# One-core cross-attention and routed FFN: first product transposed, slots by a matmul per batch, units of 32 tokens on four column tiles

## What is computed

```python
x = x + _L0_xattn_ref(_layernorm(x), ctx_1024, ctx_1024, ctx_1024)
#   x1 = x @ w1.T; x2 = x @ v1.T; h = gelu_tanh(x1) * x2; return h @ w2     (w1 = v1 = w2 = ctx)
x = x + _L0_ffn_ref(_layernorm(x), router_w, w1, b1, w2, b2)
#   assign = argmax(x @ router_w); w = sigmoid(logit of assign)
#   out = (gelu(x @ w1[assign] + b1[assign]) @ w2[assign] + b2[assign]) * w
```

## Time and profile before

| | |
|---|---|
| median of 3 runs | 468.7 us (468.23 to 469.79) |
| profiled execution, its span | 468.6 us |
| TensorE busy | 315.6 us (67%) |
| VectorE, ScalarE, GpSimd busy | 93.7, 84.7, 79.0 us |
| granted TensorE clock, mean | 0.842 of 2.4 GHz |
| moved by DMA | 102.18 MB, mean 218 GB/s |

### The profile page before, as it was taken

One profiled execution on the slowest core, in us unless ns is written; L12 is line 12 of the kernel. 1 busy time (PEld: TensorE's weight loads), 2 busy tenths in 40 slices (PEclk: granted clock), 3 DMA queues, 4 the chain that ended last, 5 costly groups with the idle time before them and its releaser, 6 DMA issues.

```text
span 468.6 us, 5970 instructions
## 1 busy us (share of the span) xinstructions
PE 315.6 (67%) x1840; PEld 156.7 (33%) x1841; DVE 93.7 (20%) x289; ACT 84.7 (18%) x129; POOL 79.0 (17%) x132
## 2 busy tenths in 40 slices
PE   3797897797793359585796617628777096577871
PEld 1353453353352214331353203213334042232441
DVE  1243443443335210100111000100111011010210
ACT  2120120121020012221044002102122021040410
POOL 0000000000001310313224220320323203202241
PEclk9998988998896576987999687875989587887998
DMA  8698987988879593697718754874785555000000
GB/s 293 215 328 259 300 268 238 284 261 279 293 285 322 157 396 160 232 344 259 285 59 293 296 191 181 325 257 182 277 308 213 200 183 197 26 3 20 20 25 5
DMA packets 19762, 102.18 MB, mean 218 GB/s; under 512 B 3757, under 2 KB 4013, under 8 KB 10480
## 3 DMA queue, kind: packets, MB, share of 16 engines
q1 hardware_dynamic: 16592, 96.22, 57.9%
q0 software_dynamic: 3104, 4.94, 3.3%
HBM read 99.23 MB, written 6.04 MB: 225 GB/s over the span
## 4 chain that ended last, share of the span: by engine, by line
PE 53%; issue 22%; DMA 19%; DVE 3%; SPq 1%; POOL 0%; ACT 0%; DVEq 0%; POOLq 0%; ACTq 0%
PE bank L502 17%; DMA area<-in_ctxT_a 16%; PE bank L466 12%; PE bank L476 7%; PE bank L369 7%; PE bank L495 3%; DMA b1s<-in_b 3%; PE bank L486 2%; PE bank L397 2%; PE bank L455 2%; DMA work<-t_rows,id_tok 1%; PE bank L384 0%; PE bank L447 0%; DVE tn L602 0%; PE bank L363 0%
## 5 line engine op out<-in xcount | busy, mean ns | idle before, releaser
L466 PE MATMUL bank<-W_early,work 128*64 128x512 f32 x128 | 44.1, 852 | 40.7 <-issue 39.9
L369 PE MATMUL bank<-area,xnT 128*100 128x338 f32 (+1 forms) x128 | 54.2, 577 | 17.6 <-DMA area<-in_ctxT_a 17.0
L502 PE MATMUL bank<-W_early,work 128*64 128x256 f32 x512 | 62.1, 397 | 0.0
L809 POOL DMA_INDIRECT out<-work,at_out x21 | 21.6, 1027 | 205.5 <-DVE work L728 205.5
L476 PE MATMUL bank<-W_early,work 128*32 128x256 f32 x256 | 24.5, 495 | 45.0 <-issue 45.0
L397 PE MATMUL bank<-work,hidT 128*100 128x512 f32 (+1 forms) x96 | 47.3, 604 | 0.6 <-ACT hidT L563 0.6
L502 PEld LDWEIGHTS bank<-W_early,work 128*64 128x64 f32 x512 | 36.8, 143 | 24.9 <-issue 9.7
L737 DVE COPY work<-bank 128x256 f32<-128x256 f32 (+1 forms) x21 | 11.6, 552 | 167.5 <-PE bank L466 97.6
L369 PEld LDWEIGHTS bank<-area,xnT 128*100 128x100 f32 x128 | 25.1, 207 | 44.5 <-issue 23.0
L586 ACT ACTIVATE work<-work 128x512 f32<-128x512 f32 x21 | 13.3, 631 | 140.1 <-DVE work L741 140.1
L466 PEld LDWEIGHTS bank<-W_early,work 128*64 128x64 f32 x128 | 12.2, 195 | 67.2 <-issue 66.1
(11 more groups left out here) (95 smaller groups left out, 260.1 us busy)
## 6 DMA issues: line engine op xcount, KB each, us to landing
W_early<-in_w SPq DMA_DIRECT2D x52, 1024.0 KB, 7.0
work<-in_ctx_main SPq DMA_DIRECT2D x8, 1280.0 KB
area<-in_ctxT_a SPq DMA_DIRECT2D x8, 768.0 KB, 12.4
work<-in_w SPq DMA_DIRECT2D x6, 1024.0 KB, 9.0
area<-in_w SPq DMA_DIRECT2D x6, 1024.0 KB, 9.2
area<-in_ctxT_b SPq DMA_DIRECT2D x8, 676.0 KB, 11.5
xw_rows<-xw SPq DMA_DIRECT2D x8, 200.8 KB
area<-in_x SPq DMA_DIRECT2D x8, 200.0 KB
```

What stands on the lines that cost most here:

```text
L369: last = nc.tensor.matmul((p_xa, p_xb)[part][0:T, 0:hi - lo], xnT[:, k, :], ctxTs[part][:, k, :], start=(k == 0), stop=(k == KD - 1))
L466: last = nc.tensor.matmul(p_h[BLK * h:BLK * h + BLK, :], pairT[:, k, BLK * par:BLK * par + BLK], W1[slot][:, k, D * h:D * h + D], start=(k ...
L502: last = nc.tensor.matmul(p_y[BLK * h:BLK * h + BLK, 0:HD], hT[:, 2 * (c % 4) + c // 4, :], W2[slot][:, c, HD * h:HD * h + HD], start=Fals ...
L809: nc.gpsimd.indirect_dma_start(out_halves, bass.IndirectOffsetOnAxis(ap=at_out[par][:, :], axis=0), y_out[par], None, bounds_check=bound_x ...
```

## The change

- **First product transposed.** Context columns are stationary and the 100 tokens move (`hidden`): the product comes out as context x tokens, in the form in which `attention` needs it. The transposes of the hidden rows and their copies go.
- **Context in thirds of a ring.** `ctxT_part` and `ctx_part` have three buffers each, every one for half a batch's context. Two weight pieces stand between the loads of each batch.
- **Raw x in the rows.** Per batch one tensor `rows` takes x after attention with mean, inverse deviation and gate; each token is four pieces of 128 columns. Logits are computed from x itself with a centred router (`rc`), the gate from the logit times the inverse deviation. Units normalise after the gather.
- **Slot table by a matmul per batch.** `place_rows` writes two one-hot matrices, `slots` adds tok_hot.T x slot_hot (100 x 128 by 100 x 400) to the table in PSUM.
- **Units of 32 tokens**, each on four column tiles in both layers. A gather brings 128 pieces (32 tokens x 4), VectorE normalises them and transposes 32 x 32 blocks, also the result of the first layer (`turn`), and TensorE returns the residual by an identity. There is one form only: no branch on the size.
- **Four early units**, for experts 0 to 3, take tokens of batches 0 to 6; between them the last batch is routed. Then each expert has one unit that always runs (`must`) and further ones in a loop (`more`); all experts are unrolled.
- **Weights.** Five slots as before, in four pieces; the loads wait for release only. Biases b2 are loaded once, broadcast.

The core of the diff, in the order SyncE, TensorE, ScalarE, VectorE, GpSimd:

```diff
-EARLY = (0, 1, 1, 1, 1, 1, 2, 3)
+XS, CS = 96, 80
 SA = 3 * P
-BLK = 64
-SMALL = 32
-MAXB = E - 1 + -(-(TOK - E + 1) // BLK)
-NCOL = MAXB + 6
-NTHR = TOK // BLK
+XR = 3
+U = 32
+Q = 4
+ROW = P + 4
+EARLY = 4
 SLOTS = 5
...
+        def units_of_experts(eng, must, more):
+            begin = 0
+            for e in range(E):
+                must(e, begin)
+                end = end_of(eng, e)
+                with eng.If(end > begin):
+                    with eng.Fori(begin, end) as f:
+                        more(e, f, begin)
+                begin = end
+            return begin
...
+            early = iter([(e, piece) for e in range(SLOTS - 1) for piece in range(4)])
             for b in range(NB):
+                if 2 * b + 3 < 2 * NB:
+                    sp.wait_ge(s_xps[0], b + 1)
+                    load_ctxT(2 * b + 3)
+                load_w(*next(early))
+                if 2 * b + 4 < 2 * NB:
+                    sp.wait_ge(s_xps[1], b + 1)
+                    load_ctxT(2 * b + 4)
+                if b == 1:
+                    sp.dma_start(b1s[:, :, :], b1).then_inc(s_bias, 16)
+                    sp.wait_ge(s_b2q, 32)
+                    for j in range(Q):
+                        sp.dma_start(b2s[U * j:U * j + U], b2_q[j].unsqueeze(0).to_broadcast([U, E, P + 1])
+                                     ).then_inc(s_bias, 16)
+                if 2 * b + 3 < 2 * NB:
+                    sp.wait_ge(s_att0, b + 1)
+                    load_ctx(2 * b + 3)
+                load_w(*next(early))
+                if 2 * b + 4 < 2 * NB:
+                    sp.wait_ge(s_att, b + 1)
+                    load_ctx(2 * b + 4)
+                if b + 3 < NB:
+                    sp.wait_ge(s_x2, b + 1)
+                    load_x(b + 3)
+            sp.wait_ge(s_xps[1], NB)
+            load_w(SLOTS - 1, 0)
...
+            for e in range(SLOTS, E):
+                sp.wait_ge(s_w1_used, e - SLOTS + 1)
+                load_w(e, 0)
+                load_w(e, 1)
+                sp.wait_ge(s_w2a_used, e - SLOTS + 1)
+                load_w(e, 2)
+                sp.wait_ge(s_w2b_used, e - SLOTS + 1)
+                load_w(e, 3)
...
+            def hidden(b, c):
+                n = 2 * b + c // 3
+                if c % 3 == 0:
+                    pe.wait_ge(s_T[n % 3], t_count(n))
+                bank_c = (p_xa, p_xb)[c // 3]
+                at0 = T * (c % 3)
+                for k in range(KD):
+                    last = nc.tensor.matmul(bank_c[0:CW[c], at0:at0 + T],
+                                            ctxT_part(n)[:, k, P * (c % 3):P * (c % 3) + CW[c]], xnT[:, k, :],
                                             start=(k == 0), stop=(k == KD - 1))
+                if c % 3 == 2:
+                    last.then_inc(s_xps[c // 3], 1)
...
+            def slots(b):
+                pe.wait_ge(s_slot, b + 1)
+                nc.tensor.matmul(p_tab if b < NB - 1 else p_tab_last, tok_hot[:, :],
+                                 slot_hot[:, :, :].rearrange("p e n -> p (e n)"),
+                                 start=(b % (NB - 1) == 0), stop=(b >= NB - 2)).then_inc(s_tabps, 1)
...
+            def first_layer(v, e, first, used):
+                slot, landed = e % SLOTS, 16 * (e // SLOTS) + 16
+                pe.wait_ge(s_xT, v)
+                pe.wait_ge(s_hc, v)
                 for k in range(KD):
                     if first and k % 2 == 0:
+                        pe.wait_ge(s_w[slot][k // 2], landed)
+                    for q in range(Q):
+                        last = nc.tensor.matmul(p_h[U * q:U * q + U, 0:2 * P], xT[:, U * k:U * k + U],
+                                                W1[slot][:, k, :].rearrange("p (c q l) -> p q c l", c=KF, q=Q)[:, q],
+                                                start=(k == 0), stop=(k == KD - 1), tile_position=(0, U * q))
+                        if used and k == 0 and q == 0:
+                            last.then_inc(s_w1_used, 1)
+                last.then_inc(s_h, 1)
+                pe.wait_ge(s_rT, v)
+                pe.wait_ge(s_res, v)
+                for q in range(Q):
+                    last = nc.tensor.matmul(p_r[U * q:U * q + U, 0:P], rT[:, U * q:U * q + U], ident,
+                                            start=True, stop=True, tile_position=(0, U * q))
+                last.then_inc(s_r, 1)
...
+            def second_layer(v, e, used):
+                slot, landed = e % SLOTS, 16 * (e // SLOTS) + 16
+                pe.wait_ge(s_act, v)
+                pe.wait_ge(s_yo, v)
                 for c in range(KF):
+                    if c % 4 == 0:
+                        pe.wait_ge(s_w[slot][2 + c // 4], landed)
+                    for q in range(Q):
+                        last = nc.tensor.matmul(p_y[U * q:U * q + U, 0:P], hT[:, c, :],
+                                                W2[slot][:, c, P * q:P * q + P],
+                                                start=(c == 0), stop=(c == KF - 1), tile_position=(0, U * q))
+                        if used and c == KF // 2 and q == 0:
+                            last.then_inc(s_w2a_used, 1)
                 last.then_inc(s_y, 1)
...
+            def must(e, begin):
+                v = pe.snap(begin + (EARLY + e + 1))
+                first_layer(v, e, e >= EARLY, e > 0)
+                second_layer(v, e - 1 if e > 0 else EARLY - 1, e > 0)
+            def more(e, f, begin):
+                v = pe.snap(f + (EARLY + e + 2))
+                first_layer(v, e, False, False)
+                second_layer(v, e, False)
...
+            def gelu_unit(v, v1):
+                act.wait_ge(s_hb, v)
+                if v1 is not None:
+                    act.wait_ge(s_y, v1)
+                nc.scalar.activation(hT[:, :, :], hb[:, :].rearrange("p (c t) -> p c t", c=KF), ACT.Gelu
+                                     ).then_inc(s_act, 1)
...
+            def fetch(j, v, row, index, e):
+                nc.vector.tensor_scalar(tb[:, :], row[:, 0:P], row[:, P + 1:P + 2], row[:, P + 2:P + 3],
+                                        ALU.subtract, ALU.mult).then_inc(s_tb, 1)
+                dve.wait_ge(s_tb, v)
+                nc.vector.transpose(xT[:, :], tb[:, :]).then_inc(s_xT, 1)
+                nc.vector.transpose(rT[:, :], row[:, 0:P]).then_inc(s_rT, 1)
+                nc.vector.tensor_copy(lin[:, bass.ds(ring(j), 1)], index)
...
+            def residual(j, v, row, e):
+                dve.wait_ge(s_r, v)
+                nc.vector.scalar_tensor_tensor(out=res[:, bass.ds(ring(j) * ROW, P + 1)], in0=b2s[:, e, :],
+                                               scalar=row[:, P + 3:P + 4], in1=p_r, op0=ALU.mult, op1=ALU.add
+                                               ).then_inc(s_res, 1)
...
+            def finish(j, v):
+                dve.wait_ge(s_y, v)
+                dve.wait_ge(s_yfree, v)
+                dve.wait_ge(s_res, v)
+                at0 = ring(j) * ROW
+                to = j % 2 * P if isinstance(j, int) else dve.snap(j % 2) * P
+                nc.vector.scalar_tensor_tensor(out=y[:, bass.ds(to, P)], in0=p_y[:, 0:P],
+                                               scalar=res[:, bass.ds(at0 + P, 1)], in1=res[:, bass.ds(at0, P)],
                                                op0=ALU.mult, op1=ALU.add).then_inc(s_yo, 1)
...
+            def turn(v):
+                dve.wait_ge(s_h, v)
+                nc.vector.transpose(hb0[:, :], p_h[:, 0:KF * U]).then_inc(s_hc, 1)
+            def add_bias(v, v1, e):
+                dve.wait_ge(s_hc, v1)
+                dve.wait_ge(s_act, v)
+                nc.vector.tensor_tensor(hb[:, :].rearrange("p (h n t) -> p h n t", h=2, n=4),
+                                        hb0[:, :].rearrange("p (h n t) -> p h n t", h=2, n=4),
+                                        b1s[:, e, :].rearrange("p (n h) -> p h n", h=2).unsqueeze(3
+                                                               ).to_broadcast([P, 2, 4, U]), ALU.add).then_inc(s_hb, 1)
...
+            def must(e, begin):
+                v, j = dve.snap(begin + (EARLY + e + 1)), dve.snap(begin + (EARLY + e))
+                dve.wait_ge(s_must[e], 16)
+                at0 = NB32 * (e + 1) + (e < EARLY)
+                fetch(j, v, frow[:, e, :], tab[:, at0:at0 + 1], e)
+                finish(dve.snap(begin + (EARLY + e - 2)), v)
+                turn(v)
+                add_bias(v, dve.snap(begin + (EARLY + e + 2)), e)
+                residual(j, v, frow[:, e, :], e)
...
+            def put_out(j, v, par):
+                if isinstance(j, int):
+                    at0 = j % 4
+                else:
+                    at0 = pool.snap(j % 4)
+                pool.wait_ge(s_yo, v)
+                nc.gpsimd.tensor_copy(at[par][:, :], lin[:, bass.ds(at0, 1)]).then_inc(s_at, 1)
+                pool.wait_ge(s_at, v)
+                nc.gpsimd.indirect_dma_start(out_q, bass.IndirectOffsetOnAxis(ap=at[par][:, :], axis=0),
```

(19 more changed lines are left out.)

1170 lines of the change are left out of this document (536 added, 634 removed).

## The result

The new kernel takes **354.1 us** (median of four runs, 351.5 to 358.0) against 469.3 of the kernel before on the same chip: a ratio of **0.751, 95% interval 0.746 to 0.756**. The profiled execution has a span of 351.0 us. The forecast was 341 (312 to 382). All medians here are over all runs of a kernel, while the ratios leave out runs over 1.5% above the fastest of their kernel; by this stricter rule the medians would be 353.1 us for the new kernel, 322.3 in experiment 1, 336.7 in 3, 348.0 in 7, 321.1 in 9, and within 0.5 us of those given in the others.

A forecast was written before the change was run, and what follows sets the result against it. The prediction saw serial waits in attention and table stages, and TensorE's far branches in the units, as the bound. Attention 128, table and early units 28.5, units 154, branches 18 and tail 12 sum to 341 us, range 312 to 382.

The forecast's parts named there:

- attention stage ends: Attention stage: 41.7 MB at 340 GB/s, 123 us, plus 5 us of start, gives 128 us; bounds 116 to 155.
- to the first regular first layer: Table and early units: early gather, then VectorE's pace through four units and last routing, 28.5 us, to 156.5.
- 27 distances, undisturbed: Regular units: VectorE's chain of 5.1 us sets the period, taken as 5.5 (5.0 to 6.4); 28 units, 154 us.
- what skips add: Unit stage: eight far TensorE branches, 3.5 us less 1.3 covered by queued matmuls, 18 us; bounds 0 and 38.
- last unit and tail: End of kernel: after the last unit, second layer 1.9 plus 9.4 us, 12 with its wait.
- Forecast A: Whole kernel: the forecast sum holds, 330 to 352 us; chance 0.45.
- Rival D: Attention stage: deeper buffers don't raise the DMA rate, 276 GB/s, stage ends at 156, total 369 us; chance 0.11.
- text's signs of being wrong: First layers wait for gathers or weights, or VectorE's list after the last attention product takes over 25 us.
- C: Units: TensorE's instruction stream bounds; records at 60 ns (6.4 us a unit) and branches at 4.8, 386 us; chance 0.24.
- Weights: Weight loads: expert 5 starts at 167, eleven experts at 370 GB/s land by 292 us, hidden with some 15 us spare.
- Rival B: Units: weights bound, 307 us, beside VectorE's chain at 5.0 with branches covered, 308; interfering up to 325; chance 0.18.
- E: Units: slower than before; scatter landing of 18 us makes units over 9.7 us, total above 468.7; chance 0.02.

The follow-up runs named there:

- experiment 1: New kernel with TensorE's stream written out (known unit counts as constants, no branch, loop or count load), other engines unchanged: 325.5 us.
- experiment 3: Kernel before with only TensorE's stream written out (known blocks and sizes as constants, no branches), other engines as they were: 337.1 us, ratio 0.722.
- experiment 7: New kernel with the fifth slot's weights issued only after the gathers of the early units have landed: 351.4 us, ratio 0.746.
- experiments 9: New kernel with TensorE's stream written out, plus a spare VectorE transpose of 0.45 us behind each regular unit's first layer: 321.5 us, ratio 0.688.
- Experiment 6: New kernel with the sixteen early weight pieces moved behind the attention stage: 348.2 us, ratio 0.744.
- Experiments 2: New kernel with the streams of TensorE, VectorE, ScalarE and GpSimd all written out (known counts, no branches): 321.7 us, ratio 0.687.
- experiment 11: New kernel with TensorE's stream written out, second layers cut from 128 to 64 columns: 320.2 us, ratio 0.686.
- 12: New kernel with TensorE's stream written out, every other chunk of the second layers left out (64 fewer instructions a unit): 316.4 us, ratio 0.680.
- experiment 5: Kernel before with the block-size branch removed on all engines, every block in the 64-token form, no knowledge of the routing: 377.2 us, ratio 0.802.
- experiment 4: Kernel before with TensorE's stream written out and SyncE's four waits for landings of the previous weight halves removed: 338.2 us, ratio 0.723.

## Why the prediction was right or wrong

The sum was 128 + 28.5 + 154 + 18 + 12; taken apart at the last unit's first layer it can be laid beside the trace.

| | predicted | measured |
|---|---|---|
| attention stage ends | 128 | 130.1 |
| to the first regular first layer | 28.5 | 34.1 |
| 27 distances, undisturbed | 27 x 5.5 = 148.5 | 27 x 4.66 = 125.9 |
| what skips add | 18 | 42.0 |
| last unit and tail | 5.5 + 12 | 18.9 |

**Forecast A: 10 us short of the span, the units right by luck, with two errors that cancel.** The measured median lies 2 us above A's own range, well inside the whole one. By the distances the unit's period was sized too long by 0.84 us, and the skips at less than half: seven at 6.0 us, not eight at 2.2. -22.6 and +24.0 leave +1.4. If only what experiment 1 took away is put down to the skips, they are 27.5 (+9.5) and the rest 140.4 (-8.1): less wrong each, and cancelling as well.

**Attention stage: right in what bounds it, its end partly by luck.** 41.7 MB, full share, 359 GB/s where 340 was taken. Those 41.7 MB were moved by 119.5 us (a mean of 349 GB/s from the start), when the last part of the transposed context landed, 8.5 us before the sum's 128; then came 10.6 us of the last batch's products, which were no term of it. Experiment 6 shows the stage bound by DMA, with TensorE 11 us below (12.8 us a batch, where the sum gave 11.7). Rival D is out: the deeper buffers did raise the rate.

**Table and early units: +5.6.** The step that failed is the start: "some 3 us for the early gather". The gather reads rows from memory that the last batch has first to be written to; this write, 6.4 us behind weight pieces, was no term of the sum, and the gather took 5.65, not 3.5. From the first early unit on, 24.6 us were predicted (the terms given add up to 24.9) and 25.4 measured.

**Period: the mechanism holds for a part of the units, size off.** VectorE's list from the end of a first layer to the next tokens' transposes takes 1.8 to 2.7 us in most units and 3.5 in two, where 3.0 was summed, and the 0.4 added for control and clock wasn't needed. TensorE waits for it before 10 of the 28 first layers; others start with TensorE's own layers back to back, 3.9 us apart, or behind a stop. Experiments 2 and 9 show that it yields to others over the whole stage. Of the text's signs of being wrong, one came up once: the first layer at 210.34 waited for its gather (5.54 us, landed at 209.6), of which VectorE stood still for 1.5.

**Second layer: C's first half is out.** Its 64 records take

```profile
148.20 1.95 PE bank L398 x64
```

so four column tiles run at 30 ns a record, half of the 60 that C took, and with half the columns (experiment 11, in the timeline: start, us)

```profile
171.10 1.08 PE L409 MATMUL bank<-W_early,hT 128*32 128x64 f32 x64
```

it is the columns that set it. The Trainium skill's "TensorE: Matmul & The Clock Gate" (What happens when you issue a matmul) has about 62 ns as what the sequencer may spend on a matmul. The prediction put that figure on each of the 64 records, 4.0 us, which is out at once. That the 64 records of the whole form come to 61 ns a pair, an fp32 matmul being two, would agree; the 34 ns a pair of the half form doesn't, and decides: no such bound here.

**Skips: the term that was mis-sized, and the second half of C the nearest of the rivals.** The branch itself was foreseen, and rather lower than its 3.5 us: its 16 instances sum to 16.3 us, those of the seven skips to 14.6, 2.1 each (L239 and L226 of the earlier trace rows sum to 53 and 21). What failed is "less 1.3 that queued matmuls cover", a figure that no run shows, and the thought that the wait ends with the branch. TensorE stops again inside the next layers (2.80 us at 181.4), and the lower clock follows; since these stops go with the branches in experiment 1, the code behind the target isn't there either. The bound of 38 us for it, kept in the range, lies between the 27.5 of experiment 1 and the 42 of the distances. The rule of the Trainium skill ("Runtime: NRT & Kernel Launch", Instruction fetch mechanics) that branching breaks the sequential prefetch fits the stops at the branches and behind them. Its remark there that crossing a block is mostly hidden agrees with experiment 3, where straight code kept TensorE busy 40 of 40 us; whether the short stops of experiment 1, in straight code too, are such crossings no run here shows.

**Weights: hidden, as said, and later.** They land at 305 us, not 292, since expert 5's loads start at 175 instead of 167 and SyncE waits for slots again from 209 on. By then six units were still to start; no first layer waited for them. Rival B's bound is neared only in the written-out versions. E's scatter isn't in the chain of the new kernel's units; in experiments 9 and 12 it is. E's own condition has a slip: at a landing of 18 us, 9.7 a unit, the sum comes to 458 us, and only from about 19 us of landing above 468.7.

**What the text didn't weigh.** It named the far branch as the old kernel's trouble, yet argued the gain from attention, table and early start, and put the units at 172 us by a fresh sum. The runs put it the other way round: the change gained 115 us, writing out TensorE's stream alone in the old kernel gains 129, deleting the branch on the size 91. All that was built for the array and the DMA is worth 12 us once TensorE is written out in both.

## What to carry to other kernels

A branch on TensorE costs by the code that it leaves and lands in, also after it has been decided: add up the sequencer's long branches, the stops inside layers behind them and the clock they cost. Try first to delete a special case (a second form of code for small blocks) before tuning either form. To size such a stall, write the stream out with known counts; it took one run to show 129 us. And before believing a chain that names transfers, look at the busy shares of the same window: at equal pace it names either side.

## What was not expected of the hardware

- Only TensorE waits at branches: in the new kernel 0.08 to 4.7 us, against 34 to 69 ns on VectorE, ScalarE and GpSimd for the same branch. Where the code jumped over got smaller (experiment 5), all 16 stayed at 0.35 us or less; the jump back over a group of five experts took 7.4 us, the same jump on VectorE at most 0.07.
- Weight pieces of 1 MB alone arrive at 413 to 419 GB/s on this single core, where weights of before came at 341 to 367. With at most two in flight they came at 368 in one window of experiment 3, without that limit at 415 in the same window of experiment 4; over the whole unit stage both had about 360.
- A write of 206 KB by GpSimd takes 4.2 us to land without weight pieces in flight and 6.7 with them (medians of experiment 6 and of the new kernel), and the first early gather behind them 5.65 (experiment 7: 2.73 without them).

**Open.** What the short stops in straight code are wasn't settled: they follow the number of instructions, but change from run to run. Nor was it settled what binds the written-out versions, the weights or the scatters; a third buffer for the results of units would tell. Nor was it tried to put the old kernel's one form on the new attention stage, or to leave only a part of the early weight pieces in the attention stage, since with none of them the early units wait for weights.
